# A two-layer graph kernel: VectorE's step of the first edge layer in another order, and the first bias as one bf16 product

## The chip, the cores and the metric

The kernel runs on one core of a Trainium2 chip. The metric is the device time of one execution in microseconds. The profile is of one execution; its records name TensorE (PE, with its weight loads as PEld), VectorE (DVE), ScalarE (ACT), GpSimd (POOL) and SyncE (SP).

## The reference, cut to what matters

There are 50000 nodes with 64 features and 50000 edges, sorted by their destination `dst`. Two layers follow one another, each behind a layer norm and a relu, and each added to its input:

```
h  = relu(layernorm(x))
Wh = h @ W + b
Wr, Wc = Wh[src], Wh[dst]
sim = dot(Wr, Wc) / max(|Wr| * |Wc|, 1e-8)
base = edge_weight * softplus(c0 * edge_weight_n2 + c1) * (src != dst)
x = x + scale * (m0 * segsum(base * relu(sim) * Wc, src) + m1 * segsum(base * -relu(-sim) * Wc, src) + m2 * Wh)
h  = relu(layernorm(x))
msgs = mlp(concat(h[dst], h[src]))           # 128 -> 128 -> 64, relu between
x = x + mlp(concat(h, segsum(msgs, dst)))
```

Here m0, m1 and m2 are the softmax of three coefficients, and `segsum` adds rows that have one index. Because `dst` is sorted, the destination rows of 128 consecutive edges lie close together; the source rows lie anywhere.

## The kernel before, in words

The kernel has six stages. **Preparation** (`prepare`, 0 to 26 us) loads the edge numbers and the weights, turns them so that edges lie on partitions, and works out the edges' base weights on VectorE in a chain of linked small instructions. Its last block ends when all engines have ended.

The **first node stage** (`node_phase0`, 27 to 229 us) goes through 49 blocks of 1024 nodes. For each, SyncE loads x; VectorE, GpSimd and ScalarE make the layer norm (sum, mean, centring on GpSimd in L496, squares on ScalarE in L503, root in L512, five eighths of h on VectorE in L528 and three on ScalarE in L522); TensorE transposes h in four pieces (L646); ScalarE copies the result (L623); TensorE then multiplies: the bias enters as a product of a row of ones with eight copies of b (`ones_row`, `b_rows`, both fp32, L655), on which eight records of fp32 products with W accumulate (L657). ScalarE copies Wh out (L629), VectorE adds it to x (L596), SyncE stores both. Between its centrings GpSimd gathers the x rows of a quarter of the sources ahead (L606).

The **first edge layer** (`edge_*` with layer 0, 230 to 1395 us) goes through 98 blocks of 512 edges, in 4 slots of buffers. GpSimd gathers the Wh rows of the sources with an indirect DMA for each 128 edges (L1222, three in each block, since every fourth block has its rows from the x rows gathered ahead) and later adds the weighted sums to the table of x with four indirect DMAs (L1247). Every scatter waits for the one before. The destination rows come without a gather: SyncE loads windows of 384 rows (L1195), VectorE makes a one-hot matrix in three instructions from 512 fp16 positions (L1273), and TensorE multiplies it with the window (`find`, L1485). VectorE compares the two ends (L1306), marks equal sources within the block (`match`, L1290), works out where the sums go (`address`, L1349, L1354) and the weights (`weigh`, L1316 to L1324). The messages are split into three bf16 parts, by turns on ScalarE (L1430, L1434) and VectorE (`leave`, L1337, and `low`, L1342), and TensorE adds the messages of equal sources (L1533). ScalarE copies these sums (L1440) for the scatter.

The order of each engine's work is written out in a list `parts`: for each block number the function `rounds_of_blocks` issues every part in the order of the list, on the block number plus the part's offset. A part waits on semaphores for what it needs, and everything behind it on the engine waits with it. On VectorE in the first edge layer, `ahead` makes the indices (L1266) that the gather reads, once the gather four blocks back has landed, and then the one-hot; `compare` waits for the gathered rows of its block. `norm_ahead` does the layer norm of the rows gathered ahead, a quarter of a slot group at a time; the bias for these rows is again a product (L1552).

The other stages, which the diff does not touch, are a second layer norm (to 1535 us), the second edge layer (to 2074 us) and the last node stage.

Of the kernel before, what the change touches and what calls it, by code (L numbers as in the profile page):

```python
# [6 lines left out]
BF16 = mybir.dt.bfloat16  # L7
# [5 lines left out]
P = 128  # L13
N = 50000
E = 50000
D = 64
# [95 lines left out]
def build(nc, x, src, dst, edge_weight, edge_weight_n2, W, b, deg_coeff, coeff_param, scale_param,  # L112
          mW1, mb1, mW2, mb2, uW1, ub1, uW2, ub2, out):
    ctx = ExitStack()
    with ctx:
        def sb(name, shape, dt=FP32):
            return ctx.enter_context(nc.sbuf_tensor(name, shape, dt))

        def table(name, shape):
            return nc.dram_tensor(name, shape, FP32, kind="Internal").ap()  # L120


        tabs = {name: table(name, [ROWS, D]) for name in ("wh", "x1", "h1", "agg")}

        tabs["ends"] = table("ends", [2, TILES, P])
        tabs["rel"] = nc.dram_tensor("rel", [TILES, P], FP16, kind="Internal").ap()

        c = dict(
            sems=Semaphores(nc),

            gathered=[[ctx.enter_context(nc.semaphore(f"e{layer}_gathered{s}")) for s in range(ESLOTS)]
                      for layer in range(2)],
            ahead_in=ctx.enter_context(nc.semaphore("n0_ahead_in")),
            mask_ready=ctx.enter_context(nc.semaphore("mask_ready")),
            added=[[ctx.enter_context(nc.semaphore(f"e{layer}_added{s}")) for s in range(ESLOTS)]
                   for layer in range(2)],
            ident=sb("ident", [P, P]),
            not_before=sb("not_before", [P, G * P]),
            near=sb("near", [1, 1], INT32),
            first_i=sb("first_i", [1, TILES], INT32),  # L140
            in_window=sb("in_window", [P, WK]),
            in_span=sb("in_span", [P, SPAN], FP16),
            rel_col=sb("rel_col", [P, GROUPS, G]),
            at_i=sb("at_i", [1, TILES], INT32),
            zeros=sb("zeros", [P, SPARE * D]),
            eps_ln=sb("eps_ln", [P, 1]),
            trash=sb("trash", [P, G]),
            w_blk=sb("w_blk", [P, 2 * D]),
            b_rows=sb("b_rows", [1, R, D]),
            ones_row=sb("ones_row", [1, P]),  # L150
            mw1=sb("mw1", [P, DH]), mw1_odd=sb("mw1_odd", [P, DH]), mb1_col=sb("mb1_col", [P, 1]),
            mw2=sb("mw2", [P, D]), mb2_row=sb("mb2_row", [P, D]),
            uw1=sb("uw1", [P, DH]), ub1_col=sb("ub1_col", [P, 1]),
            uw2=sb("uw2", [P, D]), ub2_row=sb("ub2_row", [P, D]),
            mix=sb("mix", [P, 3]),
            edge_f=sb("edge_f", [P, 3, GROUPS, G]),
            edge_i=sb("edge_i", [P, 2, GROUPS, G], INT32),
            bank=[ctx.enter_context(nc.psum_tensor(f"bank{i}", [P, 512], FP32)) for i in range(8)],
        )
        prepare(nc, c, tabs, src, dst, edge_weight, edge_weight_n2, W, b, deg_coeff, coeff_param,  # L160
                scale_param, mW1, mb1, mW2, mb2, uW1, ub1, uW2, ub2)
        first_phases(nc, c, tabs, x, sb)
        c["sems"] = Semaphores(nc)
        edge_phase(nc, c, tabs)
        c["done"].give_back()
        c["sems"] = Semaphores(nc)
        node_phase2(nc, c, tabs, out)


def prepare(nc, c, tabs, src, dst, edge_weight, edge_weight_n2, W, b, deg_coeff, coeff_param,  # L170
            scale_param, mW1, mb1, mW2, mb2, uW1, ub1, uW2, ub2):

    with ExitStack() as ctx:
# [25 lines left out]
        soft = [sb(f"soft{i}", [P, TC + 1]) for i in range(3)]  # L199
        differ = sb("differ", [P, TC])  # L200
        dc = sb("dc", [P, 2])
        cp = sb("cp", [P, 3])
        cps = [sb(f"cps{i}", [P, 3]) for i in range(4)]

# [11 lines left out]
        with nc.Block() as block:  # L216
# [29 lines left out]
            def _(act):  # L246
# [4 lines left out]
                          (cp[:], row(coeff_param).to_broadcast([P, 3])),  # L251
                          (deg[:, TC:TC + 1], row(scale_param).to_broadcast([P, 1])),
                          (c["w_blk"][0:D, 0:D], W), (c["w_blk"][D:2 * D, D:2 * D], W),
                          (c["b_rows"][:], row(b).unsqueeze(1).to_broadcast([1, R, D]))]
                mlps = [(c["mw1_odd"][0:D, :], mW1[D:2 * D, :]), (c["mw1_odd"][D:2 * D, :], mW1[0:D, :]), (c["mw1"][:], mW1), (c["mw2"][:], mW2), (c["uw1"][:], uW1), (c["uw2"][:], uW2),
                        (c["mb1_col"][:], col(mb1)), (c["ub1_col"][:], col(ub1)),
                        (c["mb2_row"][:], row(mb2).to_broadcast([P, D])),
# [18 lines left out]
            def _(pool):  # L276
# [12 lines left out]
                steps.mark(nc.gpsimd.iota(in_window_i[:], pattern=[[1, WK]], base=0, channel_multiplier=WK))  # L289
                steps.mark(nc.gpsimd.iota(in_span_i[:], pattern=[[1, SPAN]], base=0, channel_multiplier=0))  # L290
                steps.link(nc.gpsimd.iota(trash_i[:], pattern=[[P, G]], base=TRASH, channel_multiplier=1))
                nc.gpsimd.memset(c["ones_row"][:], 1.0).then_inc(pool_made, 1)
                nc.gpsimd.affine_select(out=c["ident"][:], in_=c["ident"][:], compare_op=ALU.not_equal,
                                        fill=1.0, base=0, pattern=[[-1, P]],
                                        channel_multiplier=1).then_inc(pool_made, 1)
# [40 lines left out]
            def _(dve):  # L336
# [46 lines left out]
                                                   ALU.mult, ALU.add))  # L383
                steps.link(nc.vector.tensor_copy(soft[0][:, TC:TC + 1], deg[:, TC:TC + 1]))
                nc.vector.scalar_tensor_tensor(soft[2][:], soft[0][:], -1.0, soft[0][:], ALU.mult, ALU.max).then_inc(soft_in, 1)

                steps.link(nc.vector.tensor_reduce(cps[3][:, 0:1], cp[:], AX.X, ALU.max))
                nc.vector.tensor_scalar(cps[0][:], cp[:], cps[3][:, 0:1], None, ALU.subtract).then_inc(mix_in, 1)
# [150 lines left out]
def node_phase0(nc, c, tabs, x, slots):  # L539
# [99 lines left out]
    def tensor(pe):  # L639
# [10 lines left out]
        def multiply(s, k):  # L650
            pe.wait_ge(hT_ready, count(s, k))
            if has(s, k, 2):
                pe.wait_ge(wh_ready, count(s, k, 2))

            nc.tensor.matmul(wh_bank[s % 2][:], c["ones_row"][:], c["b_rows"][:].rearrange("p r d -> p (r d)"), start=True, stop=False)  # L655
            for q in range(R // 2):
                last = nc.tensor.matmul(wh_bank[s % 2][:, q * P:(q + 1) * P], hT[s][:, q * P:(q + 1) * P],  # L657
                                        c["w_blk"][:], start=False, stop=q == R // 2 - 1)
            last.then_inc(wh_done, 1)
# [596 lines left out]
def edge_vector(nc, dve, c, t, layer, near):  # L1256
# [2 lines left out]
    def of_group(a, s, k):  # L1259
        return a[:, :, bass.ds(ESLOTS * k + s, 1), :].rearrange("p w a j -> p w (a j)")  # L1260

    def ahead(s, k):

        if has(s, k, ESLOTS, ESLOTS):
            t.all_gathered(dve, s, k - 1, near)
        nc.vector.tensor_copy(t.ids[s][:], of_group(c["edge_i"], s, k)).then_inc(t.ids_ready, 1)  # L1266
        if not near:
            return
        t.numbers(dve, s, k, near)
        if has(s, k, ESLOTS, ESLOTS):  # L1270
            dve.wait_ge(t.found, count(s, k, ESLOTS, ESLOTS))
# [102 lines left out]
                                           ALU.max, ALU.mult).then_inc(a.h_ready, 1)  # L1374

    if layer == 0:
        parts = [(-3, leave), (0, ahead), (-3, low), (-2, compare), (-1, match), (-2, address), (-2, weigh)]
        parts += [(0, norm_ahead)] * near
    else:
        parts = [(-3, low), (0, ahead), (-1, match), (-2, address), (-2, bias), (-2, leave)]  # L1380
    rounds_of_blocks(dve, parts, ESLOTS, GROUPS)


# [81 lines left out]
def edge_tensor(nc, pe, c, t, layer, near):  # L1465
# [82 lines left out]
    def multiply_ahead(s, k):  # L1548
        a = t.ahead
        if a.due(s, k, 3):  # L1550
            pe.wait_ge(a.hT_ready, k + 1)
            nc.tensor.matmul(bank[AHEAD_BANK][:, 0:G * D], c["ones_row"][:], c["b_rows"][:, 0:G, :].rearrange("p r d -> p (r d)"),  # L1552
                             start=True, stop=False)
            for q in range(G // 2):
                last = nc.tensor.matmul(bank[AHEAD_BANK][:, q * P:(q + 1) * P], a.hT[:, q * P:(q + 1) * P], c["w_blk"][:],
                                        start=False, stop=q == G // 2 - 1)
            last.then_inc(a.wh_done, 1)
# [188 lines left out]
```

## Time and profile before

| | |
|---|---|
| median of 3 runs | 2294.8 us (2292.69 to 2296.01) |
| the profiled execution | 2299.84 us, its span 2298.1 us |
| busy in the span | PE 71%, PEld 60%, DVE 69%, ACT 37%, POOL 71% |
| granted TensorE clock, mean | 0.703 |
| moved by DMA | 273.15 MB, mean 119 GB/s |

A row of a timeline gives the start and the duration of one instruction, or of several of one line that follow each other (x3), in microseconds from the span's start, then the engine, the line of the kernel, the operation and what is written from what. In brackets stands the idle time of the engine ahead of it and who ended it; "issue" is time in which the engine waited for nothing that the profile shows. The duration of one fp32 product is recorded as two matmuls.

### The profile page before, as it was taken

What the parts mean: (1) busy time and instruction counts of PE and PEld (TensorE: products, weight loads), DVE (VectorE), ACT (ScalarE), POOL (GpSimd) and SP (SyncE); (2) the same over time, 40 slices, a digit from 0 to 9 for tenths busy, and PEclk for the clock granted to TensorE, in tenths of its full rate; (3) what the DMA queues carried; (4) which work ended last, traced back from release to release, by engine and by line L of the source; (5) the groups of instructions that cost most, each with busy time, mean ns of one, the idle gap of its engine ahead of it and who ended that gap; (6) DMA issues with size and microseconds to landing.
All of it is one profiled execution on the core that took longest, in us unless ns stands there. A gap on an engine that the chain in (4) does not pass through costs nothing. (4 is left out here: it accounts for less than half of the span.)

```text
span 2298.1 us, 58041 instructions
## 1 busy us (share of the span) xinstructions
PE 1640.3 (71%) x16196; PEld 1389.6 (60%) x16196; DVE 1596.7 (69%) x5830; ACT 858.3 (37%) x3189; POOL 1629.4 (71%) x1364
## 2 busy tenths in 40 slices
PE   3987866676666666666667640019999999998998
PEld 2554765665566566666566540018999999984544
DVE  5787765666666656666666655967999999994554
ACT  2666322322332222322232223643333333334665
POOL 5778688888888888888888877547777777742232
PEclk9889555555555555555555555559999999999999
DMA  3666644444444444444444424665555555525664
GB/s 98 206 230 232 148 86 87 88 88 88 88 84 91 85 84 82 94 82 88 88 87 88 88 21 120 219 180 129 126 125 126 125 125 125 125 54 154 190 184 145
DMA packets 342566, 273.15 MB, mean 119 GB/s; under 512 B 144834, under 2 KB 273514, under 8 KB 342484
## 3 DMA queue, kind: packets, MB, share of 16 engines
q1 hardware_dynamic: 259028, 233.22, 35.4%
q0 software_dynamic: 81536, 38.61, 15.1%
q8 instruction: 34, 0.56, 0.1%
q10 hardware_dynamic: 1920, 0.37, 0.1%
q14 instruction: 48, 0.39, 0.1%
HBM read 206.69 MB, written 65.34 MB: 118 GB/s over the span
## 5 line engine op out<-in xcount | busy, mean ns | idle before, releaser
L1247 POOL DMA_INDIRECT x<-e_sums,e_to x392 | 632.8, 1614 | 133.6 <-issue 118.5
L1485 PE MATMUL bank<-e_window,e_onehot 128*128 128x64 f32 x2352 | 522.1, 421 | 16.2 <-DMA e_window<-wh 16.2
L1485 PEld LDWEIGHTS bank<-e_window,e_onehot 128*128 128x128 f32 x2352 | 512.3, 333 | 16.7 <-issue 16.7
L896 POOL DMA_INDIRECT e_near_source<-h,e_near_ids x392 | 394.2, 1006 | 130.4 <-issue 92.0
L1533 PE MATMUL bank<-e_parts,e_same 128*128 128x64 bf16 x2940 | 173.0, 241 | 390.5 <-DVE e_parts L1342 390.5
L1533 PEld LDWEIGHTS bank<-e_parts,e_same 128*128 128x128 bf16 x2940 | 160.0, 130 | 411.2 <-issue 411.2
L1222 POOL DMA_INDIRECT e_ends<-wh,e_ids x296 | 305.7, 1033 | 96.3 <-issue 86.2
L1306 DVE SCALAR_TENSOR_TENSOR e_prod<-e_ends,bank 128x64 f32<-128x64 f32 x392 | 63.1, 217 | 353.3 <-DMA e_ends<-wh,e_ids 353.3
L1006 PE MATMUL bank<-e_near_to_edge,e_near_window 128*64 128x128 f32 x2352 | 152.6, 280 | 163.8 <-DMA e_near_window<-h 163.8
L1391 ACT ACTIVATE e_sq<-e_ends 128x64 f32<-128x64 f32 x392 | 95.1, 243 | 442.3 <-DMA e_ends<-wh,e_ids 442.3
L1006 PEld LDWEIGHTS bank<-e_near_to_edge,e_near_window 128*64 128x64 f32 x2352 | 129.0, 139 | 169.6 <-DVE e_near_to_edge L917 164.6
L1290 DVE SCALAR_TENSOR_TENSOR e_same<-e_owners,e_ef,bank 128x512 bf16<-128x512 f32 (+3 forms) x392 | 191.5, 545 | 7.3 <-DVE e_ef L1281 4.6
L979 ACT ACTIVATE e_near_hid<-bank,mb_col 128x512 f32<-128x512 f32 x98 | 67.3, 687 | 331.6 <-PE bank L1026 331.6
L1623 POOL TENSOR_TENSOR n_x<-n_x,ub_row 128x512 f32<-128x512 f32 x49 | 62.2, 1269 | 178.3 <-DMA n_x<-x 178.3
L955 DVE TENSOR_TENSOR agg_sb<-bank,agg_sb 128x256 f32 x392 | 163.4, 417 | 1.4 <-DVE agg_sb L955 0.6
L1050 PEld LDWEIGHTS bank<-e_near_parts,e_near_to_node 128*128 128x128 bf16 x4704 | 150.3, 98 | 17.9 <-DVE e_near_to_node L924 4.2
L1050 PE MATMUL bank<-e_near_parts,e_near_to_node 128*128 128x64 bf16 x4704 | 153.2, 193 | 3.9 <-DVE e_near_parts L939 3.9
L1273 DVE TENSOR_SCALAR e_onehot<-e_rel,in_window 128x512 f32<-128x512 f16 x294 | 133.6, 510 | 15.1 <-DMA e_rel<-rel 15.1
L1644 ACT ACTIVATE n_hid<-bank,ub_col 128x512 f32<-128x512 f32 x98 | 102.9, 1154 | 76.9 <-PE bank L1698 76.8
L1430 ACT CAST e_parts<-e_msgs 128x256 bf16<-128x256 f32 x98 | 39.7, 405 | 242.9 <-DVE e_msgs L1324 242.9
L917 DVE TENSOR_SCALAR e_near_to_edge<-e_near_rel,in_window 128x512 f32<-128x512 f16 x294 | 125.2, 484 | 4.9 <-DMA e_near_rel<-rel 4.9
L924 DVE TENSOR_SCALAR e_near_to_node<-in_span,rel_col 128x512 bf16<-128x512 f16 x392 | 125.9, 363 | 0.0
(167 smaller groups left out, 3340.0 us busy)
## 6 DMA issues: line engine op xcount, KB each, us to landing
e_window<-wh SPq DMA_DIRECT2D x392, 96.0 KB
e_near_window<-h SPq DMA_DIRECT2D x392, 96.0 KB
e_owners<-ends SPq DMA_DIRECT2D x98, 256.0 KB, 3.0
n_x<-x SPq DMA_DIRECT2D x98, 256.0 KB, 2.8
n_x<-in_x_dram SPq DMA_DIRECT2D x49, 256.0 KB, 2.8
wh<-n_wh SPq DMA_DIRECT2D x49, 256.0 KB, 2.1
x<-n_x SPq DMA_DIRECT2D x49, 256.0 KB, 2.4
e_rel<-rel SPq DMA_DIRECT2D x98, 128.0 KB, 3.4
```

Source lines behind the costliest of these rows:

```text
L896: pool.indirect_dma_start(out=t.source[s][:, j, :], out_offset=None, in_=tabs["h1"], in_offset=bass.IndirectOffsetOnAxis(ap=t.ids[s][:, j: ...
L917: nc.vector.tensor_scalar(t.to_edge[s % 2][:, w, :], t.rel[s][:], c["in_window"][:, w:w + 1], None, ALU.is_equal).then_inc(t.to_edge_ready, 1)
L924: nc.vector.tensor_scalar(t.to_node[s % 2][:, j, :], c["in_span"][:], c["rel_col"][:, bass.ds(ESLOTS * k + s, 1), j:j + 1].rearrange("p a ...
L955: nc.vector.tensor_tensor(here, sums, here, ALU.add).then_inc(t.agg_ready, 1)
L1006: last = nc.tensor.matmul(bank[s % 2][half:half + D, j * P:(j + 1) * P], t.window[s][:, j, w, :], t.to_edge[s % 2][:, w, j * P:(j + 1) * P ...
L1050: last = nc.tensor.matmul(to[:, at:at + D], t.to_node[s % 2][:, j, b * P:(b + 1) * P], t.parts[s % 2][:, part, j, :], start=part == 0, sto ...
L1222: pool.indirect_dma_start(out=t.ends[s][:, j, at, :], out_offset=None, in_=gathered_tab, in_offset=bass.IndirectOffsetOnAxis(ap=t.ids[s][: ...
L1247: pool.indirect_dma_start(out=added_tab, out_offset=bass.IndirectOffsetOnAxis(ap=t.to[s][:, j:j + 1], axis=0), in_=t.sums[s][:, j, :], in_ ...
L1273: last = nc.vector.tensor_scalar(t.onehot[s][:, w, :], t.rel[s][:], c["in_window"][:, w:w + 1], None, ALU.is_equal)
L1290: nc.vector.scalar_tensor_tensor(t.same[s][:, same_block(j, j):same_block(j, G - 1) + 1, :].rearrange("p b i -> p (b i)"), t.owners[s][:, ...
L1485: last = nc.tensor.matmul(bank[FIND_BANKS[s]][:, j * D:(j + 1) * D], onehot, window, start=w == 0, stop=w == WK - 1)
L1533: last = nc.tensor.matmul(bank[6 + s % 2][:, i * D:(i + 1) * D], t.same[s][:, same_block(j, i), :], t.parts[s][:, part, j, :], start=j == ...
```

## The change

VectorE's list for the first edge layer is reordered. `ahead` is cut in two parts, `indices` and `lookup` (the one-hot). Seen from the block m whose one-hot is made in a step, the parts were: second half of the split `leave` of m-3, indices and one-hot of m, `low` of m-3, `compare` m-2, `match` m-1, `address` m-2, `weigh` m-2. They become: indices of m+2, `leave` and `low` of m-3, `compare` m-2, `match` m-1, one-hot of m, `address` m-2, `weigh` m-2. The unrolled rounds before and after the loop become one more each. The other engines' lists stay.

The bias of the first layer, fp32 in one row on a K of 1, is cut into three bf16 parts on three partitions; it enters with one bf16 product on a K of 3, the copies for the 8 (or 4) rows coming from a broadcast in the operand. Seven linked instructions in the preparation make the three parts.

```
-            b_rows=sb("b_rows", [1, R, D]),
-            ones_row=sb("ones_row", [1, P]),
+            b_parts=sb("b_parts", [3, D], BF16),
+            ones_rows=sb("ones_rows", [3, P], BF16),
...
+                dve.wait_ge(pool_made, 8)
+                row_of = lambda i: c["ident"][0:3, i:i + 1]
+                steps.link(nc.vector.tensor_copy(b_high[:], b_rows[:]))
+                steps.link(nc.vector.scalar_tensor_tensor(b_left[:], b_rows[:], 1.0, b_high[:], ALU.mult, ALU.subtract))
+                steps.link(nc.vector.tensor_copy(b_mid[:], b_left[:]))
+                steps.link(nc.vector.scalar_tensor_tensor(b_low[:], b_left[:], 1.0, b_mid[:], ALU.mult, ALU.subtract))
+                steps.link(nc.vector.tensor_scalar(b_first[:], b_high[:], row_of(0), None, ALU.mult))
+                steps.link(nc.vector.scalar_tensor_tensor(b_two[:], b_mid[:], row_of(1), b_first[:], ALU.mult, ALU.add))
+                steps.link(nc.vector.scalar_tensor_tensor(c["b_parts"][:], b_low[:], row_of(2), b_two[:], ALU.mult, ALU.add))
...
-            nc.tensor.matmul(wh_bank[s % 2][:], c["ones_row"][:], c["b_rows"][:].rearrange("p r d -> p (r d)"), start=True, stop=False)
+            nc.tensor.matmul(rows(wh_bank[s % 2][:]), c["ones_rows"][:], c["b_parts"][:].unsqueeze(1).to_broadcast([3, R, D]),
+                             start=True, stop=False)
...
-    def ahead(s, k):
-
+    def indices(s, k):
         if has(s, k, ESLOTS, ESLOTS):
             t.all_gathered(dve, s, k - 1, near)
         nc.vector.tensor_copy(t.ids[s][:], of_group(c["edge_i"], s, k)).then_inc(t.ids_ready, 1)
-        if not near:
-            return
+
+    def lookup(s, k):
         t.numbers(dve, s, k, near)
...
-        parts = [(-3, leave), (0, ahead), (-3, low), (-2, compare), (-1, match), (-2, address), (-2, weigh)]
-        parts += [(0, norm_ahead)] * near
+        parts = [(0, indices), (-5, leave), (-5, low), (-4, compare), (-3, match)] + [(-2, lookup)] * near
+        parts += [(-4, address), (-4, weigh)] + [(-2, norm_ahead)] * near
...
-            nc.tensor.matmul(bank[AHEAD_BANK][:, 0:G * D], c["ones_row"][:], c["b_rows"][:, 0:G, :].rearrange("p r d -> p (r d)"),
-                             start=True, stop=False)
+            nc.tensor.matmul(rows(bank[AHEAD_BANK][:, 0:G * D]), c["ones_rows"][:],
+                             c["b_parts"][:].unsqueeze(1).to_broadcast([3, G, D]), start=True, stop=False)
```

## Rows read from the trace of the kernel before

**Rows 1.** The page: the span, and the granted clock in 40 slices.
```profile
span 2298.1 us, 58041 instructions
...
PEclk9889555555555555555555555559999999999999
```

**Rows 2.** Stages: stretch, its length, busy time of each engine, granted clock, DMA share, GB/s.
```profile
94.00:107.00 13.00, 12.65 (x41) 8.38 (x41) 9.47 (x19) 6.60 (x20) 9.78 (x10) 0.50 0.61 204
...
125.00:141.00 16.00, 16.00 (x50) 10.31 (x49) 11.10 (x23) 8.38 (x25) 11.27 (x11) 0.50 0.62 209
142.00:218.00 76.00, 62.89 (x318) 37.89 (x316) 71.05 (x131) 56.52 (x160) 61.58 (x57) 1.00 0.71 235
500.00:1300.00 800.00, 516.66 (x3832) 489.26 (x3833) 503.08 (x2503) 236.90 (x1440) 654.07 (x480) 0.50 0.47 87
```

**Rows 3.** Timeline of the first node stage at the low clock level.
```profile
130.88 1.06 PE L646 MATMUL bank<-ident,n_h 128*128 128x128 f32 x4
...
131.87 2.07 PE L655 MATMUL bank<-b_rows,ones_row 1*128 1x512 f32 x2
...
133.65 0.83 ACT L522 ACTIVATE n_h<-n_xc,n_rstd 128x64 f32<-128x64 f32 x3
```

**Rows 4.** Timeline of the first node stage at the high clock level.
```profile
159.91 0.83 ACT L522 ACTIVATE n_h<-n_xc,n_rstd 128x64 f32<-128x64 f32 x3
...
160.84 0.63 PE L646 MATMUL bank<-ident,n_h 128*128 128x128 f32 x4 [0.49 <-DVE n_h L528]
...
164.23 0.65 PE L646 MATMUL bank<-ident,n_h 128*128 128x128 f32 x4 [0.63 <-ACT n_h L522]
```

**Rows 5.** Timeline of TensorE: transposes of blocks 1, 7 and 48.
```profile
42.76 1.09 PE L646 MATMUL bank<-ident,n_h 128*128 128x128 f32 x4 [2.36 <-ACT n_h L522]
...
71.94 1.06 PE L646 MATMUL bank<-ident,n_h 128*128 128x128 f32 x4
...
218.21 0.63 PE L646 MATMUL bank<-ident,n_h 128*128 128x128 f32 x4
```

**Rows 6.** Groups of GpSimd, 500 to 1300 us: count | busy us, mean ns | idle before.
```profile
L1247 POOL DMA_INDIRECT x<-e_sums,e_to x273 | 440.6, 1614 | 83.2 <-issue 83.2
L1222 POOL DMA_INDIRECT e_ends<-wh,e_ids x207 | 215.1, 1039 | 63.1 <-issue 60.9 <-DMA x<-e_sums,e_to 2.1
```

**Rows 7.** Timeline: a one-hot and the second gather of a block.
```profile
1062.71 1.27 DVE L1273 TENSOR_SCALAR e_onehot<-e_rel,in_window 128x512 f32<-128x512 f16 x3
...
1063.62 1.55 POOL L1222 DMA_INDIRECT e_ends<-wh,e_ids  x1 [0.30 <-issue]
```

**Rows 8.** Timeline: a scatter under a one-hot, and gathers and scatters without.
```profile
849.09 1.27 DVE L1273 TENSOR_SCALAR e_onehot<-e_rel,in_window 128x512 f32<-128x512 f16 x3
...
850.02 1.77 POOL L1247 DMA_INDIRECT x<-e_sums,e_to  x1 [0.30 <-issue]
852.09 1.01 POOL L1222 DMA_INDIRECT e_ends<-wh,e_ids  x1 [0.30 <-issue]
...
854.68 0.94 POOL L1222 DMA_INDIRECT e_ends<-wh,e_ids  x1 [0.30 <-issue]
855.93 1.62 POOL L1247 DMA_INDIRECT x<-e_sums,e_to  x1 [0.30 <-issue]
...
859.74 1.55 POOL L1247 DMA_INDIRECT x<-e_sums,e_to  x1 [0.30 <-issue]
```

**Rows 9.** Timeline: the last instruction of VectorE in the preparation.
```profile
25.61 0.22 DVE L404 TENSOR_SCALAR mix<-cps,soft 128x3 f32<-128x3 f32 x1
```

**Rows 10.** Timeline: the first sums of the edge layer, bf16 products of 64 columns.
```profile
255.54 1.76 PE L1533 MATMUL bank<-e_parts,e_same 128*128 128x64 bf16 x30 [0.16 <-DVE e_parts L1342]
```

**Rows 11.** Timeline: a compare behind its gathered rows, and a scatter.
```profile
822.06 0.22 DVE L1306 SCALAR_TENSOR_TENSOR e_prod<-e_ends,bank 128x64 f32<-128x64 f32 x1 [4.89 <-DMA e_ends<-wh,e_ids]
...
832.74 1.62 POOL L1247 DMA_INDIRECT x<-e_sums,e_to  x1 [0.30 <-issue]
```

**Rows 12.** Timeline: the first scatter.
```profile
258.58 1.64 POOL L1247 DMA_INDIRECT x<-e_sums,e_to  x1 [7.68 <-DVE e_to L1354]
```

More of the change, by code:

```diff
@@ L201, in prepare @@
         dc = sb("dc", [P, 2])
+        b_rows, b_left, b_low, b_first, b_two = (sb(f"b_{n}", [3, D]) for n in ("rows", "left", "low", "first", "two"))
+        b_high, b_mid = sb("b_high", [3, D], BF16), sb("b_mid", [3, D], BF16)
         cp = sb("cp", [P, 3])
@@ L253, in _ @@
                           (c["w_blk"][0:D, 0:D], W), (c["w_blk"][D:2 * D, D:2 * D], W),
-                          (c["b_rows"][:], row(b).unsqueeze(1).to_broadcast([1, R, D]))]
+                          (b_rows[:], row(b).to_broadcast([3, D]))]
                 mlps = [(c["mw1_odd"][0:D, :], mW1[D:2 * D, :]), (c["mw1_odd"][D:2 * D, :], mW1[0:D, :]), (c["mw1"][:], mW1), (c["mw2"][:], mW2), (c["uw1"][:], uW1), (c["uw2"][:], uW2),
@@ L291, in _ @@
                 steps.link(nc.gpsimd.iota(trash_i[:], pattern=[[P, G]], base=TRASH, channel_multiplier=1))
-                nc.gpsimd.memset(c["ones_row"][:], 1.0).then_inc(pool_made, 1)
+                nc.gpsimd.memset(c["ones_rows"][:], 1.0).then_inc(pool_made, 1)
                 nc.gpsimd.affine_select(out=c["ident"][:], in_=c["ident"][:], compare_op=ALU.not_equal,
@@ L1376, in edge_vector @@
     if layer == 0:
-        parts = [(-3, leave), (0, ahead), (-3, low), (-2, compare), (-1, match), (-2, address), (-2, weigh)]
-        parts += [(0, norm_ahead)] * near
+        parts = [(0, indices), (-5, leave), (-5, low), (-4, compare), (-3, match)] + [(-2, lookup)] * near
+        parts += [(-4, address), (-4, weigh)] + [(-2, norm_ahead)] * near
     else:
-        parts = [(-3, low), (0, ahead), (-1, match), (-2, address), (-2, bias), (-2, leave)]
+        parts = [(-3, low), (0, indices), (-1, match), (-2, address), (-2, bias), (-2, leave)]
     rounds_of_blocks(dve, parts, ESLOTS, GROUPS)
```

## The prediction

> **What bounds the kernel now.** I read the page first: the granted clock by slices changes level around two long stages [rows 1], so the bound changes by stage. The table of stages comes next [rows 2], then the timeline of single steps. Three facts carry the argument.
>
> First node stage, 39 to 226 us. TensorE starts a block with four transposes (L646), then two products for the bias (L655), then eight for W (L657). At its low clock level (1.2 GHz) these three groups touch (transposes at 130.88, bias from 131.87 for 2.07 us), TensorE is busy 16.00 of 16.00 us [rows 2, 3] and the block lasts 4.86 us (29.18 us between turns 42.76 and 71.94, six blocks [rows 5]). At the high level (2.4 GHz) blocks come 164.23 - 160.84 = 3.39 us apart and TensorE idles before each; there a loop decides: transposes, ScalarE's copy of them, its root, square and copy of Wh, then three pieces of h, next transposes [rows 4]. The granted clock is 0.50 in two stretches of 13 and 16 us [rows 2]; a third has no record, but its transposes take 1.06 us instead of 0.63, from 42.76 to 71.94 [rows 4, 5].
>
> First edge layer, 230 to 1395 us. GpSimd never waits for data: from 500 to 1300 us its 273 scatters and 207 gathers take 440.6 + 215.1 us, and the 146.3 us between them is the 0.30 us before each instruction, "issue" [rows 6]. That is 802 us of 800: GpSimd is the bound, 11.7 us a block (273 / 4 = 68.3 blocks in 800 us). TensorE is busy 516.66 of 800 and VectorE 503.08 [rows 2].
>
> GpSimd's durations do depend on VectorE. A second gather in a row takes 1.55 us where a one-hot (L1273) runs into its start [rows 7], free ones 1.01 to 0.94; a scatter takes 1.77 us under a one-hot, free ones 1.62 for the first of four down to 1.55 [rows 8]. The means of 1614 and 1039 ns [rows 6] against free runs of four scatters and three gathers (means 1.575 and 0.973, their first and last in [rows 8]) are 4 x 0.039 + 3 x 0.066 = 0.35 us a block, 35 us over 98 blocks.
>
> **The change part by part.**
>
> Preparation. Seven linked VectorE instructions on 3x64 elements are added ahead of the softmax of the coefficients. A linked small one takes 0.22 us [rows 9], a part of the one-hot with 128x512 elements 1.27 / 3 = 0.42 [rows 7]; bounds 1.1 to 3.0 us, I take 1.6, nearest to the small one. The last one of VectorE ends the stage (25.83 [rows 9]; no other engine works later, and the node stage's loads follow it), so nothing hides the addition: **+1.6**. ScalarE's logarithm moves along with it. The wider constant transfer is waited for at the same place as before, and GpSimd's eight constants are long made.
>
> Bias product in the node stage. Two fp32 products of 512 columns go (2.07 us at the low level [rows 3]) and one bf16 product of 512 columns comes. The trace has bf16 products of 64 columns, 30 in 1.76 us [rows 10], so 8 x 0.059 = 0.47 us at the low level; bounds 0.2 and 1.0 (half of the pair). TensorE's low-level block is then 4.86 - 2.0 + 0.47 = 3.3 us and no longer the bound. What is late next is the loop: ScalarE's last piece of h ends 133.65 + 0.83 - 130.88 = 3.60 us after the transposes began [rows 3], and the next transposes start 0.1 us behind such an end (159.91 + 0.83 = 160.74, then 160.84 [rows 4]): 3.70 us. At the upper bound of the price TensorE needs 3.9 us, at the lower the loop holds. At the high level the loop stays, so nothing is gained there.
> From turn 42.76 to turn 218.21 there are 47 blocks [rows 5]. Low-level time is 29.2 + 13 + 16 = 58.2 us, 12 blocks at 4.86; the other 35 take 117.3 us, 3.35 each. If the clock is low for as many blocks as before: 12 x (4.86 - 3.70) = **-14**. If it is never low: 12 x (4.86 - 3.35) = -18. If it is low throughout: 47 x 3.70 - 175.5 = -1.6. I take the first: the clock fell while TensorE was kept in work by the loop, rose while it ran without a gap, and the change makes the low-level block (3.3 of 3.7 us busy) not much emptier; nothing in the trace says which way that moves it.
> The Trainium skill, "TensorE: Matmul & The Clock Gate" (Part 1), says that the default state is throttled and activity releases it. By that rule a less busy TensorE would stay low more: the sum would lose most of the 14. The trace agrees in part: the edge stage, TensorE 65% busy, stays at 0.50 [rows 2]; but gap-free work from 42.76 to 71.94 stayed low too.
>
> Bias product of the rows prepared ahead, once in four blocks of the edge stage: about 1 us less TensorE, hidden by its idle third: 0.
>
> New order of VectorE's step. For block m the step was: split of m-3, indices and one-hot of m, second split, then a wait for the gathered rows, compare m-2, match m-1, address, weigh. Now the wait comes first (the indices of m+2 reuse the buffer that the gather of m-2 reads), then splits, compare, match, one-hot of m, address, weigh. VectorE waits 4.89 us in such a step now, ahead of its compare [rows 11], so its work of some 7.4 us (503.08 / 68.3) still fits 11.7. What moves: indices are two blocks earlier; the one-hot is later by about one block (from ahead of the landing to 4.1 us behind it: indices 0.2, two splits and ScalarE's cast between them 1.3, compare 0.6, match 2.0); sums on TensorE are later by 6 us. Who waits for that? The scatter of m-3. Landing at 822.06; then, after the change, splits till 823.4, products 1.76 [rows 10], ScalarE's copy about as long as a small cast, 0.4: 825.6. Its scatter starts at 832.74 [rows 11]: 7 us of cover. The find products of m run 827.5 to 833 and are wanted by the compare 20 us later. SyncE's loads of owners and windows wait for match and one-hot four blocks back, over two blocks ahead of their use: 0. GpSimd's queue has no new wait; its wait for indices goes.
> At the start of the stage GpSimd waits twice for indices, and that wait goes, but the first scatter at 258.58 [rows 12] stands behind the first sums (255.54 [rows 10]), which stand behind three finds fed by window loads; those do not move: 0.
> The one-hot meets GpSimd elsewhere. 4.1 to 5.4 us after a landing GpSimd is among its scatters in all four steps of the period, where a hit costs 0.21 (1.77 against 1.56), no longer among gathers, where it costs up to 0.58. Four hits of 0.21 and one of a split of 0.12 make 0.24 us a block instead of 0.35: -11. Bounds: no hit at all -35; each one-hot costing 0.58 +22 (98 x (0.58 - 0.35)). The positions are known to some 0.3 us only, so I take half: **-6**.
> The Trainium skill, "SBUF — State Buffer" (Who interferes with whom), says that such a VectorE operation and GpSimd's descriptor writing exclude each other for the whole instruction. One of the three one-hot parts lasts 0.42 us, and the 0.58 seen (1.55 against 0.97) is that and a little more; by the rule each one-hot could cost that, the +22 above; the scatters' 0.21 speaks against it.
>
> **Sum.** +1.6 - 14 - 6 = -18.4. The profiled execution took 2299.8 us (span 2298.1 [rows 1] and 1.7 around it), 5.0 over the median of 2294.8; on it the change would give 2281.4, on the median 2276.4, given as **2277 us**.
>
> **Rivals.**
> A, the forecast: chance 0.45, own range 2268 to 2285.
> B, the clock stays low through the node stage: -1.6 + 1.6 - 6 = -6, 2289; with the collisions unchanged 2295. For it: the edge stage at 65% never rose. Against it: TensorE stays about 0.9 busy at the low level (3.3 of 3.7). 0.25.
> C, slower: the one-hots land on instruction starts at the gather's price. +22 and, if the clock also stays low, 22 + 0 = +22: 2317; with the node stage's gain 2304. It decides from (14 - 1.6) / 98 = 0.13 us a block. For it: the gather of [rows 7]. Against it: the scatter of [rows 8], and scatters fill two thirds of GpSimd's period. 0.13.
> D, the collisions vanish: -35 + 1.6 - 14 = -47, 2247. 0.07: one-hots cover 1.3 us of 11.7 and instructions start every 1.7 us, so most hit one.
> E, the new order does not leave GpSimd free: the scatter waits for the late sums. It decides from 7 us of lateness, then 1 us costs 98 us. 0.03.
> F, the node stage is held by something else (transfers run at 235 GB/s [rows 2]) and the collisions stay: +1.6, 2296. 0.07.
>
> **How the numbers follow.** The measurement tells 0.2%, 4.6 us, from no change. Faster takes A, D and more than half of B: 0.68. Same takes the rest of B and most of F: 0.16. Slower takes C, E and a little of F: 0.16. The range goes from 2260, half way to D, to 2298, which holds B and F.
>
> **What would show it.** Right: in the node stage low-level blocks 3.7 us apart and high-level ones 3.35; first transposes 1.6 us later; GpSimd in the edge stage still with nothing but issue gaps, gathers near 0.97 and scatters near 1.6 us. Wrong: granted clock 0.50 over the whole node stage (B); mean gather above 1.1 us or scatter above 1.65 (C); idle time of GpSimd ahead of the scatter (E).

## The result, and the profile after

The changed kernel takes 2276.7 us (median of four, 2274.7 to 2282.3) against 2293.7 for the kernel before (2290.2 to 2296.0) on the same chip: a ratio of 0.9919, 95% interval 0.9896 to 0.9942. The forecast was 2277. The profiled executions took 2282.3 and 2299.8 us, each longer than the median of its kernel by about the same (5.6 and 6.1 us), so they may be set against each other: -17.5 us.

The page of the kernel after: span, granted clock in 40 slices, and three of the costliest groups (busy us, mean ns, idle before).
```profile
span 2279.8 us, 57898 instructions
...
PEclk9677555555555555555555555559999999999999
...
L1260 POOL DMA_INDIRECT x<-e_sums,e_to x392 | 630.8, 1609 | 141.6 <-issue 112.7
...
L1235 POOL DMA_INDIRECT e_ends<-wh,e_ids x296 | 289.8, 979 | 92.1 <-issue 89.1
...
L1278 DVE COPY e_ids<-edge_i 128x8 int32 (+1 forms) x98 | 18.5, 195 | 299.6 <-DMA e_ends<-wh,e_ids 298.8
```
The span is 18.3 us shorter (and 0.8 us more lies around it). The slices of the edge stage are at 5 as in [rows 1]; the first four (0 to 228 us) were 9889 and are 9677. VectorE's wait for gathered rows now stands ahead of its indices (298.8 us of 299.6), where the new list puts it.

Where the 18.3 us are, by marks read off the timelines of both (us from the span's start):

| mark | before | after | change since the mark above |
|---|---|---|---|
| transposes of block 0 | 39.31 | 40.98 | +1.67 |
| transposes of block 1 | 42.76 | 44.42 | -0.01 |
| transposes of block 48 | 218.21 | 211.30 | -8.58 |
| first scatter | 258.58 | 250.91 | -0.76 |
| last scatter | 1396.27 | 1374.31 | -14.29 |
| first find of the second layer | 1535.14 | 1513.85 | +0.67 |
| first product of its second node stage | 2078.01 | 2059.44 | +2.72 |
| end of the span | 2298.1 | 2279.8 | +0.27 |

The total came as forecast, and two large terms of it did not: the node stage gave 8.6 us instead of 14, the edge stage 14.3 instead of 6.

VectorE in the preparation: first and last of the seven new instructions, and the stage's last one.
```profile
21.69 0.17 DVE L391 CAST b_high<-b_rows 3x64 bf16<-3x64 f32 x1
...
23.20 0.27 DVE L397 SCALAR_TENSOR_TENSOR b_parts<-b_low,ident,b_two 3x64 bf16<-3x64 f32 x1
...
27.24 0.22 DVE L416 TENSOR_SCALAR mix<-cps,soft 128x3 f32<-128x3 f32 x1
```
They take 21.69 to 23.47 us, and the last instruction stands 27.24 - 25.61 = 1.63 us later than in [rows 9].

TensorE in the node stage after, at both clock levels.
```profile
44.42 1.09 PE L658 MATMUL bank<-ident,n_h 128*128 128x128 f32 x4 [2.36 <-ACT n_h L534]
...
110.03 1.08 PE L658 MATMUL bank<-ident,n_h 128*128 128x128 f32 x4
111.05 0.60 PE L667 MATMUL bank<-b_parts,ones_rows 3*128 3x512 bf16 x1
111.58 2.08 PE L670 MATMUL bank<-w_blk,n_hT 128*128 128x128 f32 x8
113.75 1.09 PE L658 MATMUL bank<-ident,n_h 128*128 128x128 f32 x4
...
136.01 0.63 PE L658 MATMUL bank<-ident,n_h 128*128 128x128 f32 x4 [1.23 <-DVE n_h L540]
...
139.28 0.63 PE L658 MATMUL bank<-ident,n_h 128*128 128x128 f32 x4 [1.23 <-DVE n_h L540]
...
211.30 1.02 PE L658 MATMUL bank<-ident,n_h 128*128 128x128 f32 x4
```
A low-level block is 113.75 - 110.03 = 3.72 us, where it was 4.86 [rows 5], and the high-level one shown 139.28 - 136.01 = 3.27 us. The bias product takes 111.58 - 111.05 = 0.53 us to the next start.

Stages of the kernel after (stretch, length, busy time of PE, PEld, DVE, ACT, POOL, granted clock, DMA share, GB/s).
```profile
104.00:128.00 24.00, 23.22 (x85) 16.86 (x85) 19.24 (x40) 16.43 (x47) 19.57 (x18) 0.50 0.68 233
132.70:147.00 14.30, 9.19 (x58) 6.58 (x59) 12.89 (x27) 10.29 (x29) 11.57 (x11) 1.00 0.70 235
142.00:205.00 63.00, 43.66 (x238) 31.76 (x238) 59.18 (x111) 45.43 (x128) 51.79 (x47) 0.87 0.70 242
500.00:1300.00 800.00, 523.42 (x3853) 493.11 (x3853) 506.87 (x2519) 243.51 (x1448) 649.02 (x485) 0.50 0.48 88
42.00:220.00 178.00, 136.15 (x634) 98.14 (x633) 148.00 (x286) 120.99 (x337) 144.43 (x133) 0.76 0.64 218
```
In [rows 2] the clock was high without a break from 142 to 218 us; now 142 to 205 has 0.87. Where the clock has no record a stretch counts as 1.00: in the kernel before that lasts to 73 us, though the transposes there take 1.06 us. So the surer witness is the duration of a block's transposes (about 1.06 us or 0.63). By it 14 of the 47 blocks from block 1 on were at the low level before, and 24 are after. In 500 to 1300 us GpSimd does 485 transfers in place of 480.

GpSimd's two groups and the one-hot in that stretch, kernel after.
```profile
L1260 POOL DMA_INDIRECT x<-e_sums,e_to x276 | 445.4, 1614 | 87.4 <-issue 79.7 <-DVE e_ids L1278 4.9 <-DMA x<-e_sums,e_to 2.8
...
L1235 POOL DMA_INDIRECT e_ends<-wh,e_ids x209 | 204.5, 978 | 63.8 <-issue 61.6 <-DMA x<-e_sums,e_to 2.1
...
L1285 DVE TENSOR_SCALAR e_onehot<-e_rel,in_window 128x512 f32<-128x512 f16 x207 | 93.3, 508 | 0.0
```
Against [rows 6]: scatters 1614 ns as before, gathers 978 instead of 1039. Some gaps are now put down to indices or an earlier scatter. Their mean ahead of a scatter rises from 0.305 to 0.317 us, and this is a wait: about every eighth block the first scatter starts 0.2 to 0.7 us late.

Timeline of the kernel after: the first scatter, a late scatter, a one-hot and the scatter and gather behind it.
```profile
250.91 1.64 POOL L1260 DMA_INDIRECT x<-e_sums,e_to  x1 [12.04 <-DVE e_to L1366]
...
724.86 1.62 POOL L1260 DMA_INDIRECT x<-e_sums,e_to  x1 [0.88 <-DMA x<-e_sums,e_to]
...
832.23 1.27 DVE L1285 TENSOR_SCALAR e_onehot<-e_rel,in_window 128x512 f32<-128x512 f16 x3
...
832.78 1.76 POOL L1260 DMA_INDIRECT x<-e_sums,e_to  x1 [0.31 <-issue]
...
838.03 0.97 POOL L1235 DMA_INDIRECT e_ends<-wh,e_ids  x1 [0.30 <-issue]
```
The indices no longer hold GpSimd at the start, and all its waiting has moved to the first scatter (12.04 us, 7.68 in [rows 12]).

From the first to the last scatter GpSimd's time adds up exactly:

| us | before | after | change |
|---|---|---|---|
| 391 scatters | 631.3 | 629.3 | -2.0 |
| 284 gathers | 293.9 | 277.9 | -16.0 |
| gaps between them | 212.5 | 216.2 | +3.7 |
| edge stage | 1137.7 | 1123.4 | -14.3 |

So the transfers themselves gave 18.0 us, and 3.7 of it went into the late scatters. Why they are late is open. They come only with the lists that begin with the indices: in e1, e3, e4 and e11 below the gaps stay at 212.3 to 212.9 us.

### The profile page after: what moved, and what is told of

Read it like the earlier page. It is cut to its first block and busy times, and to the rows that moved or that the text cites. A ratio compares the mean times of both kernels' runs of the same rounds, so it can differ in the third digit from the quotient of the medians.

```text
span 2279.8 us, 57898 instructions
## 1 busy us (share of the span) xinstructions
PE 1618.9 (71%) x16123; PEld 1388.8 (61%) x16123; DVE 1601.1 (70%) x5837; ACT 867.0 (38%) x3189; POOL 1611.8 (71%) x1364
## 5 line engine op out<-in xcount | busy, mean ns | idle before, releaser
L1260 POOL DMA_INDIRECT x<-e_sums,e_to x392 | 630.8, 1609 | 141.6 <-issue 112.7
L909 POOL DMA_INDIRECT e_near_source<-h,e_near_ids x392 | 395.0, 1008 | 130.4 <-issue 90.8
L1235 POOL DMA_INDIRECT e_ends<-wh,e_ids x296 | 289.8, 979 | 92.1 <-issue 89.1
L1545 PE MATMUL bank<-e_parts,e_same 128*128 128x64 bf16 x2940 | 173.6, 241 | 223.9 <-DVE e_parts L1354 223.9
L1545 PEld LDWEIGHTS bank<-e_parts,e_same 128*128 128x128 bf16 x2940 | 165.4, 131 | 240.4 <-issue 240.4
L1019 PE MATMUL bank<-e_near_to_edge,e_near_window 128*64 128x128 f32 x2352 | 154.2, 282 | 164.7 <-DMA e_near_window<-h 164.7
L1278 DVE COPY e_ids<-edge_i 128x8 int32 (+1 forms) x98 | 18.5, 195 | 299.6 <-DMA e_ends<-wh,e_ids 298.8
L968 DVE TENSOR_TENSOR agg_sb<-bank,agg_sb 128x256 f32 x392 | 163.3, 417 | 1.1 <-DVE agg_sb L968 0.6
L1446 ACT CAST e_parts<-e_left 128x256 bf16<-128x256 f32 x98 | 39.7, 405 | 244.4 <-DVE e_left L1349 244.4
L618 POOL DMA_INDIRECT ahead<-in_x_dram,edge_i x96 | 95.8, 997 | 45.0 <-POOLq L218 23.4
```

Source lines behind the costliest of these rows:

```text
L909: pool.indirect_dma_start(out=t.source[s][:, j, :], out_offset=None, in_=tabs["h1"], in_offset=bass.IndirectOffsetOnAxis(ap=t.ids[s][:, j: ...
L968: nc.vector.tensor_tensor(here, sums, here, ALU.add).then_inc(t.agg_ready, 1)
L1019: last = nc.tensor.matmul(bank[s % 2][half:half + D, j * P:(j + 1) * P], t.window[s][:, j, w, :], t.to_edge[s % 2][:, w, j * P:(j + 1) * P ...
L1235: pool.indirect_dma_start(out=t.ends[s][:, j, at, :], out_offset=None, in_=gathered_tab, in_offset=bass.IndirectOffsetOnAxis(ap=t.ids[s][: ...
L1260: pool.indirect_dma_start(out=added_tab, out_offset=bass.IndirectOffsetOnAxis(ap=t.to[s][:, j:j + 1], axis=0), in_=t.sums[s][:, j, :], in_ ...
L1545: last = nc.tensor.matmul(bank[6 + s % 2][:, i * D:(i + 1) * D], t.same[s][:, same_block(j, i), :], t.parts[s][:, part, j, :], start=j == ...
```

## The experiments

Each ran beside the kernel before on one chip; ratios are of medians, with the 95% interval. Experiments 1 to 4, 5 to 8 and 9 to 12 shared a chip each, so the kernels of one batch are the ones to compare; the kernel before had medians of 2296.2, 2293.3 and 2296.9 us on the three. "Node stage" is the time from the transposes of block 1 to those of block 48, "edge stage" from the first to the last scatter, in one profile each; the gathers and scatters are those from 500 to 1300 us.

| kernel | us | ratio | node stage | edge stage | gather, scatter ns |
|---|---|---|---|---|---|
| before | 2293.7 | 1 | 175.5 | 1137.7 | 1039, 1614 |
| after | 2276.7 | 0.9919 (0.9896-0.9942) | 166.9 | 1123.4 | 978, 1614 |
| e1 bias alone | 2291.3 | 0.9978 (0.9963-0.9993) | 167.6 | 1133.9 | 1029, 1612 |
| e2 order alone | 2276.0 | 0.9909 (0.9885-0.9933) | 166.4 | 1122.0 | 977, 1609 |
| e3 one-hot's place alone | 2275.5 | 0.9899 (0.9868-0.9931) | 171.0 | 1120.9 | 980, 1613 |
| e4 indices alone | 2297.3 | 1.0001 (0.9983-1.0019) | 171.4 | 1138.1 | 1008, 1641 |
| e5 one-hot last | 2294.1 | 1.0002 (0.9989-1.0016) | 164.5 | 1136.4 | 1024, 1603 |
| e6 slower one-hot | 2271.0 | 0.9896 (0.9872-0.9921) | 167.1 | 1115.4 | 979, 1593 |
| e7 filler 256 | 2271.7 | 0.9902 (0.9875-0.9929) | 162.8 | 1120.8 | 977, 1610 |
| e8 no bias | 2273.8 | 0.9907 (0.9883-0.9932) | 163.3 | 1122.5 | 976, 1611 |
| e9 parts in a wait | 2280.8 | 0.9929 (0.9915-0.9942) | 171.1 | 1121.5 | 979, 1610 |
| e10 e6, e7 and e9 | 2268.7 | 0.9884 (0.9867-0.9901) | 166.3 | 1113.3 | 980, 1588 |
| e11 slower one-hot, old order | 2277.1 | 0.9903 (0.9886-0.9920) | 183.6 | 1113.8 | 987, 1587 |
| e12 filler 512 | 2276.1 | 0.9903 (0.9888-0.9918) | 164.7 | 1121.7 | 978, 1609 |

**e1_bias_only, e2_order_only.** The change in two halves: the new bias with VectorE's old list, and the new list with the old bias.
```
e1  parts = [(-3, leave), (0, indices)] + [(0, lookup)] * near + [(-3, low), (-2, compare), (-1, match)]
    parts += [(-2, address), (-2, weigh)] + [(0, norm_ahead)] * near
```


> The bias as one bf16 product alone, with the edge layer's list as it was. Theory (two separate gains): the first transposes come 1.7 us later and the last ones 7 us earlier, the edge stage keeps its gathers at 1039 ns; in all 6 to 8 us faster than the kernel before. Rival (the bias product explains most, the edge stage only inherits it): 15 us or more faster.

> The new order alone, with the fp32 bias. Theory: the node stage is as before (last transposes near 218 us), the edge stage from first to last scatter takes 1124 us instead of 1138, the mean gather 0.98 us; in all 12 to 15 us faster. Rival (the edge gain needs the earlier end of the node stage): less than 6 us.

The order alone is worth the whole change, 0.9909 against 0.9919, and the bias alone 0.9978: 1.6 to 8.5 us of 2296. The halves add up to more than the whole, but within the intervals. So on top of the new order no gain of the bias can be seen. e1's gathers are back near the old 1039 ns, e2's stay at 977. Two expectations missed: e2 gained 20 us and not 12 to 15, and its last transposes came at 208.9 us instead of near 218, with the old bias, because only 7 of its 47 blocks were at the low level; e1 gained 4.9 us instead of 6 to 8.

**e3_lookup_mid, e4_indices_early.** The order in two halves, on the kernel before: only the one-hot behind match, the indices at their old time; and only the indices two steps ahead, the one-hot among the splits.
```
e3  [(-3, leave), (0, indices), (-3, low), (-2, compare), (-1, match)] + [(0, lookup)] * near, address, weigh
e4  [(-5, leave)] + [(-2, lookup)] * near + [(-5, low), (-4, compare), (0, indices), (-3, match)], address, weigh
```


> Kernel before with one part moved: the one-hot goes from behind the indices to behind match; indices and splits stay ahead of the wait for the gathered rows. Theory (where the one-hot meets GpSimd decides): the gathers fall to about 0.98 us, scatters stay near 1.61, 10 to 15 us faster. Rival (the indices two blocks ahead give the gain): within 4 us of the kernel before, gathers at 1.04 us.

> Kernel before with the indices made two blocks ahead, behind the compare; one-hot and splits stay where they were. Theory (indices are not waited for in the steady state): within 4 us of the kernel before, gathers near 1.04 us, only GpSimd's two waits at the start of the stage go. Rival (indices give the gain): 10 us or more faster.

e3 has all of the gain (0.9899, 21 us where 10 to 15 were expected), e4 none (1.0001). Timeline of e4: a one-hot, and a scatter that starts 0.87 us behind its start.
```profile
1079.64 1.27 DVE L1272 TENSOR_SCALAR e_onehot<-e_rel,in_window 128x512 f32<-128x512 f16 x3
...
1080.51 2.17 POOL L1247 DMA_INDIRECT x<-e_sums,e_to  x1 [0.30 <-issue]
```
2.17 us where a free one takes 1.55 [rows 8]: a scatter can pay 0.6 us as well as a gather, and 21 scatters of e4 do. From the first to the last scatter the gathers took 7.6 us less than before, the scatters 8.2 more and the gaps 0.2 less: +0.4 us. So e4's total is a zero of two parts, and its gathers (1008 ns) were not the 1040 expected; that indices two blocks earlier are worth nothing by themselves is shown by the gaps, which stay.

**e5_lookup_last.** The changed kernel with the one-hot moved on to the end of the step.
```
parts = [(0, indices), (-5, leave), (-5, low), (-4, compare), (-3, match)]
parts += [(-4, address), (-4, weigh)] + [(-2, norm_ahead), (-2, lookup)] * near
```


> Changed kernel with the one-hot moved to the end of VectorE's step, some 8 us behind a landing, when GpSimd gathers. Theory (position decides): gathers rise to 1.05 to 1.2 us, 10 to 30 us slower than the changed kernel. Rival (position does not matter, only that the splits come first): within 4 us of the changed kernel.

The gain of the order is gone, 1.0002. GpSimd's groups in e5, 500 to 1300 us.
```profile
L1260 POOL DMA_INDIRECT x<-e_sums,e_to x275 | 440.7, 1603 | 88.5 <-issue 77.9 <-DMA x<-e_sums,e_to 6.4 <-DVE e_ids L1278 4.3
...
L1235 POOL DMA_INDIRECT e_ends<-wh,e_ids x205 | 210.0, 1024 | 62.5 <-issue 59.8 <-DMA x<-e_sums,e_to 2.7
```
The gathers are hit again. From the first to the last scatter they take 12.8 us more than after, the scatters 3.0 less and the gaps 3.2 more: the edge stage is 13.0 longer. The mean gather stayed below the 1.05 us expected. So it isn't the list as such, but where the one-hot falls on GpSimd's row of transfers.

**e6_slow_onehot, e11_slow_onehot_old_order.** The same one-hot in a form with a second operand, a column of ones of the mask, which lies in PSUM: e6 on the changed kernel, e11 on the kernel before with its old order and old bias.
```
-            last = nc.vector.tensor_scalar(t.onehot[s][:, w, :], t.rel[s][:], c["in_window"][:, w:w + 1], None, ALU.is_equal)
+            last = nc.vector.scalar_tensor_tensor(t.onehot[s][:, w, :], t.rel[s][:], c["in_window"][:, w:w + 1],
+                                                  c["bank"][MASK_BANK][:, G * P - 1:G * P].to_broadcast([P, G * P]), ALU.is_equal, ALU.mult)
```


> Changed kernel with the one-hot made by a two-operand instruction whose second operand, a one from PSUM, is multiplied in; same values. Theory (the fast form of the one-hot is what blocks GpSimd): each instruction takes 0.6 to 0.8 us instead of 0.42, VectorE still fits its step, the mean scatter falls from 1614 to 1585 ns or below and the kernel is 5 to 12 us faster than the changed one. Rival (any VectorE work on SBUF slows GpSimd): scatters stay or grow, same or slower.

> Kernel before, list unchanged, with the two-operand one-hot alone. Theory (it is the fast form of the one-hot under a gather's start that costs, so the place matters only for that form): gathers fall to about 0.98 us and the kernel is 15 us or more faster without any new order. Rival (the order itself helps): gathers stay near 1.04 us, or VectorE's 0.9 us more per block makes GpSimd wait for indices, and it is the same or slower.

The groups in e6, 500 to 1300 us.
```profile
L1260 POOL DMA_INDIRECT x<-e_sums,e_to x279 | 444.4, 1593 | 87.4 <-issue 82.8 <-DVE e_ids L1278 4.6
...
L1235 POOL DMA_INDIRECT e_ends<-wh,e_ids x210 | 205.6, 979 | 64.1 <-issue 60.1 <-DMA x<-e_sums,e_to 4.0
L1285 DVE SCALAR_TENSOR_TENSOR e_onehot<-e_rel,in_window,bank 128x512 f32<-128x512 f16 x208 | 142.6, 739 | 0.0
```
The groups in e11, 500 to 1300 us.
```profile
L1247 POOL DMA_INDIRECT x<-e_sums,e_to x280 | 444.4, 1587 | 85.3 <-issue 85.3
...
L1222 POOL DMA_INDIRECT e_ends<-wh,e_ids x210 | 207.2, 987 | 64.1 <-issue 62.2 <-DMA x<-e_sums,e_to 1.8
```
Timeline of e11: the one-hot and the scatter that starts 0.94 us behind its start.
```profile
1062.99 2.06 DVE L1272 SCALAR_TENSOR_TENSOR e_onehot<-e_rel,in_window,bank 128x512 f32<-128x512 f16 x3
...
1063.93 1.55 POOL L1247 DMA_INDIRECT x<-e_sums,e_to  x1 [0.30 <-issue]
```
Timeline of the kernel after: the third scatter of a row, 0.89 us behind a one-hot's start.
```profile
646.59 1.27 DVE L1285 TENSOR_SCALAR e_onehot<-e_rel,in_window 128x512 f32<-128x512 f16 x3
...
647.48 1.86 POOL L1260 DMA_INDIRECT x<-e_sums,e_to  x1 [0.30 <-issue]
```
Timeline of e6: the third scatter of a row, 0.88 us behind.
```profile
644.39 2.05 DVE L1285 SCALAR_TENSOR_TENSOR e_onehot<-e_rel,in_window,bank 128x512 f32<-128x512 f16 x3
...
645.27 1.57 POOL L1260 DMA_INDIRECT x<-e_sums,e_to  x1 [0.31 <-issue]
```
The one-hot is 45% longer (739 ns for 508) and covers more of GpSimd's time, and the transfers that start under it take their free time: 91 in e6 are over it by 0.03 us at most, 95 of 96 in e11 by 0.02. It is not that the slower form moved the meetings elsewhere: at 0.9 us behind the start, where 42 transfers of the kernel before paid 0.21 to 0.58 us, 64 of e11 paid 0.01 or less. The old order with this form has a shorter edge stage (1113.8 us) than the new order without it (1123.4). This is what shows the cause: the form of the one-hot makes GpSimd wait, and the change of order only moved it to where it hurts less. e11's node stage was the longest of all, 183.6 us, at the old bias, and still the median is 0.9903. The median of e6 (0.9896) lies on the side of the forecast gain over the changed kernel, but the intervals overlap; its 8.0 us stand in the edge stage of one profile. Its scatters (1593 ns) stayed above the 1585 expected.
The Trainium skill, "SBUF — State Buffer" (Who interferes with whom), says that a VectorE instruction in a two-port mode shuts GpSimd out, and that one with at most one input in SBUF outside these modes does not. No trace here shows an instruction's mode. The trace agrees for the second form, with 1.55 us at 0.94 us behind the start. For the first it agrees in part: 2.17 us at 0.87, but 21 transfers of the kernel after that start 0.3 to 0.4 us behind a one-hot's start pay 0.01 to 0.09 us only.

**e7_filler, e12_filler_512, e8_no_bias.** On the changed kernel: one more bf16 product behind each block's products, into a bank that nothing reads, of 256 columns (e7) or 512 (e12); and the bias product left out (e8).
```
+            nc.tensor.matmul(c["bank"][6][:, 0:256], c["fill_w"][:], c["fill_x"][:], start=True, stop=True)
```


> Changed kernel with one more bf16 product of 256 columns on 128 rows in each block of the first node stage, whose result nothing uses. Theory (the node stage lost part of its gain because the clock is low in more of its blocks, and more activity releases it): the clock is high for more of the stage, blocks 3.3 us apart, last transposes up to 6 us earlier. Rival (the clock does not follow this activity): the low blocks grow to about 3.8 us and the stage is up to 3 us longer.

> Changed kernel whose first node stage leaves the bias product out (the bias is missing from Wh). Theory (the loop through ScalarE holds the stage, not TensorE): low blocks stay at 3.7 us, high ones at 3.3, within 3 us of the changed kernel. Rival (the product of 0.6 us is still on the path at the low level): low blocks near 3.2 us, 8 us or more faster.

> Changed kernel with an extra bf16 product of 512 columns on 128 rows a block in the first node stage instead of 256. Theory (more activity, more of the stage at the high level): high level nearly throughout, turns 1 to 48 in 158 to 163 us. Rival (it costs more than it frees): at the low level TensorE is the bound at about 3.8 us a block and the stage takes 168 us or more.

e8 is for timing alone, since the bias is missing from its Wh. The node stage in e7 (columns as for the stages above).
```profile
42.00:220.00 178.00, 113.56 (x682) 78.83 (x682) 158.49 (x286) 120.98 (x337) 144.72 (x135) 0.94 0.66 222
```
The granted clock is 0.94 in the same stretch, 0.76 in the kernel after, though the filler product is pure addition; the node stage is 162.8 us instead of 166.9. Without any bias product it is 163.3 at 0.89. The mean clock over the whole execution says the same in every run: 0.689 to 0.698 in the four of the kernel after, 0.698 to 0.709 in the twelve of e7, e8 and e12 (e10, with the filler too, lies between, at 0.693 to 0.700). Low-level blocks of e8 still come 3.63 us apart (mean of six), so no price of the bias product is left to win but through the clock. Even with 41 of 47 blocks at the high level (e7, e12) a high-level block took 3.43 to 3.45 us on average, not the 3.3 expected, and e12's stage of 164.7 us missed its 158 to 163; what holds these blocks is open. The medians (0.9902, 0.9903 and 0.9907 against 0.9919) are all on the side of a gain of about 3 to 4 us, which the intervals do not tell from none.

**e9_parts_in_wait.** The seven instructions for the parts of the bias ahead of VectorE's wait for the transposed window starts in the preparation, so that they run in it.
```
 (the seven b_* instructions and their waits)
 dve.wait_ge(first_done, 1)
```


> Changed kernel with the seven instructions that cut the bias moved ahead, into VectorE's 2 us wait for the transposed window starts. Theory (they lie bare at the end of the preparation): first transposes near 39.3 us instead of 41.0, 1.5 us faster than the changed kernel. Rival (something else is as late there): no change.

TensorE in e9: the first transposes.
```profile
39.48 1.09 PE L658 MATMUL bank<-ident,n_h 128*128 128x128 f32 x4 [20.02 <-ACT n_h L534]
```
1.5 us earlier than the 40.98 after. The median shows nothing of it: 0.9929, with a node stage of 171.1 us in the profile, at a granted clock of 0.70. The 1.5 us are shown in the trace, not in the time.

**e10_all_three.** e6, e7 and e9 together.

> Changed kernel with the two-operand one-hot, the extra product of 256 columns and the cut of the bias moved into the wait together. If the gains add up (about 6, 5 and 1.5 us): 2264 us, 12 us faster than the changed kernel. Rival (they share one cause or one engine): 2270 us, no better than the best of them.

2268.7 us, 0.9884 (0.9867 to 0.9901): the fastest of all, with the shortest edge stage (1113.3) and the start of e9 (39.35). The interval touches that of the changed kernel. It is nearer to the rival's 2270 us than to the 2264 at which the three parts would have added in full.

## Why the prediction was right in sum and wrong in two terms

**Preparation, +1.6: right.** 1.63 us at VectorE, 1.67 at the first transposes. The small linked instruction was the right row to go by.

**Node stage, -14: mechanism right, size wrong.** Low-level blocks came 3.72 us apart (forecast 3.70), high-level ones 3.27 (3.35), the bias product took 0.53 us of TensorE (0.47), and e8 (3.63 us without any product) shows that the loop, not the product, holds the block. What failed is the step "If the clock is low for as many blocks as before". The clock was low for more blocks: 24 of 47 in the kernel after, by the duration of their transposes, where I had counted 12 before and the same witness gives 14. Part of rival B happened. One profile proves little here, since the count changes from profile to profile: 14, 7, 10, 10 and 20 with the old bias (before, e2, e3, e4, e11), 24, 25, 19, 23 and 29 with the new one (after, e1, e5, e6, e9). The two groups just overlap, and their means are 12 and 24. So the clock is low in more blocks with the new product, most likely; why is open. The other fault is the ground I stood on: with the old bias this stage took 175.5, 166.4, 171.0, 171.4 and 183.6 us in five profiles (before, e2, e3, e4, e11), with the new one 166.9, 167.6, 164.5, 167.1 and 171.1 (after, e1, e5, e6, e9). The means are 173.6 and 167.4, some 6 us, with ranges that overlap; 1.7 of it go back to the preparation. e1 has 1.6 to 8.5 us for both together.

**Order: indices 0: right; waits 0: 3.7 us short.** In e4 the gaps did not change. VectorE's wait moved to the indices, and the 12.04 us ahead of the first scatter show that nothing was to be had at the start. But the argument that nobody waits for what moved was not whole: GpSimd's gaps grew by 3.7 us, nearly all of it ahead of the first scatter of about every eighth block. This is not rival E: ahead of the late scatter at 724.86 us the last sums had been copied by 718.05.

**Order: collisions -6: wrong, 18.0.** The direction and the place were right, the size was not. The step that failed is "I take half" of the -11, and under it the price "Four hits of 0.21 and one of a split of 0.12". Counted from the timelines from 280 to 1345 us, each transfer against the free time of its place in the row (gathers 1.01, 0.97, 0.94 us, scatters 1.62, 1.58, 1.56, 1.55) and only what is over it by more than 0.05 us:

| us lost | before | after |
|---|---|---|
| gathers that start while a one-hot runs | 12.4 | 0 |
| scatters that start while a one-hot runs | 9.9 | 7.4 |
| other gathers | 4.0 | 0 |
| other scatters | 2.9 | 3.5 |
| a block | 0.32 | 0.12 |

The 0.35 us a block that I had before the change was nearly right; the 0.24 that I let stand after it was twice too much. I had let each of four one-hots in four blocks hit a scatter, while after the change 31 of 91 did, for 0.24 us on average. The others ran while no transfer started, or cost one 0.05 us or less. 12.0 of the gathers' 12.4 us stood in 21 second gathers that started 0.90 us behind a one-hot's start, 0.57 each; they went, and the scatters did not pay for it.
My reason for the place was not good either. A scatter is no cheaper to hit than a gather: e4 has 21 at +0.62, and even the kernel before has two at +0.55 beside the twenty at +0.21 on which I built. What counts is at which moment of the one-hot a transfer starts, and what VectorE does behind it. The hits of 0.55 to 0.62 (before, e1, e4) all start 0.87 to 0.93 us behind the start of a one-hot that a split (`low`) follows at once. Timeline of the kernel before, the split behind the one-hot of [rows 7]:
```profile
1063.90 0.42 DVE L1342 SCALAR_TENSOR_TENSOR e_parts<-e_left,e_parts 128x256 bf16<-128x256 f32 x1
```
Where VectorE does something small next (addresses in the kernel after, indices in e5), a transfer at 0.86 to 0.91 us pays 0.27 to 0.32, and at about 1.1 0.18. A split costs by itself too: in the fourteen profiles all 247 transfers that start 0.10 to 0.20 us behind the start of one (L1337 or L1342), with no one-hot running at that moment, pay 0.10 to 0.29 us. Why 0.57 at 0.90 becomes 0.21 at 0.94 in the kernel before stays open, and no run moves the split alone.

**The rest.** After the edge stage, 3.7 us came back (the last three rows of the table). No instruction there was changed; the second layer's stages differ by such amounts among all these kernels (542.7 to 546.9 us from its first find to its second node stage in the fourteen profiles), and the cause is not known.

The hit of 2277 on 2276.7 is thus luck in good part: by e1 alone, bias and preparation gave 1.6 to 8.5 us together where 12.4 were forecast, and the order 14.3 in the edge stage (15.7 in e2) where 6 were. The two errors cancel. The range (2260 to 2298) was honest about it, the split wasn't.

## What to carry to other kernels

When GpSimd's indirect transfers are the bound, look at what VectorE does at the moments when they start. An operation there can be worth slowing down by 45% if its other form leaves GpSimd alone; try the form before the order, since an order only holds as long as the beats of both engines do. A term that hangs on a state which the trace shows in one execution, such as the granted clock, needs a second profile of the same kernel before it gets a size.

## What the runs showed of the hardware

The fast one-hot (128x512, fp16 to fp32, 0.42 us each of three) lengthens an indirect transfer that starts while it runs by 0.0 to 0.62 us according to where it starts; under the two-operand form of e6 and e11 186 of 187 such transfers were within 0.03 us of their free time. A split (128x256, fp32, two inputs, 0.42 us) lengthens a transfer that starts 0.10 to 0.20 us behind it by 0.10 to 0.29 us.

The granted clock of the node stage was higher when TensorE was given a useless bf16 product more per block (0.94, 0.96 and 0.86 in e7, e12 and e10, against 0.70 to 0.82 in the kernel after, e1, e5, e6 and e9) and also when its bias product was taken away (0.89). With the old fp32 products it was high in most blocks as well, in 27 to 40 of 47, against 18 to 28 with the new one and no filler. Busy time of TensorE alone doesn't order these. The level changes inside the stage in every profile, and what picks it is open.
